# The second graph's gathers wait for TensorE's count of finished blocks

## The reference

```python
# layer 1: neighbours' rows are summed over 200,000 edges
xn = layernorm(x);  x = x + relu(xn @ W + segment_sum((xn @ M)[src], dst))
# layer 2: the gate is a graph attention over 131,072 edges, 16 scores (4 heads x 4 experts)
h     = (xn @ W_gat).reshape(N, 4, 4)
e     = leaky_relu((h * att_src).sum(-1)[src] + (h * att_dst).sum(-1)[dst], 0.2)
alpha = softmax of e over the edges of one destination
agg   = segment_sum(h[src] * alpha, dst)          # then a layernorm, mean over heads
w     = softmax of the two best experts
out   = sum_e w_e * (gelu(xn @ W1[e] + b1[e]) @ W2[e] + b2[e]);  x = x + out
```

## Time and profile before

| | us |
|---|---|
| median of 3 runs | 3728.26 |
| lowest and highest | 3717.64 and 3728.26 |
| profiled execution, its own time | 3704.7 |
| its span, first to last instruction | 3703.5 |
| its mean granted TensorE clock | 0.87 of 2.4 GHz |

### The profile page before, as it was taken

The page is one execution under the profiler, slowest core; times in us unless marked ns, Lnnn a source line. Parts: engine busy times, 40 slices in busy tenths (PEclk is TensorE's granted clock), DMA queues, the critical chain, the costliest instruction groups (busy, mean ns, idle before and its releaser), DMA issues.

```text
span 3703.5 us, 43100 instructions
## 1 busy us (share of the span) xinstructions
PE 2698.6 (73%) x13434; PEld 1984.5 (54%) x13459; DVE 2187.1 (59%) x5820; ACT 900.4 (24%) x1563; POOL 2365.8 (64%) x2799
## 2 busy tenths in 40 slices
PE   2565767778767777677778877777867888788935
PEld 1343545555544545455555555555646766566924
DVE  6677667777765555555455554554123757566957
ACT  3000111111112222211111111111323544344623
POOL 4666666666666666556566666668886678878040
PEclk9767979889888889889899999888978989899968
DMA  9686665666666666566666666665131112122146
GB/s 290 210 259 201 185 203 182 205 205 194 192 190 195 201 199 191 184 186 200 196 206 201 206 204 203 204 203 154 29 100 35 49 38 52 32 51 55 42 142 220
DMA packets 476802, 601.20 MB, mean 162 GB/s; under 512 B 72486, under 2 KB 415390, under 8 KB 474526
## 3 DMA queue, kind: packets, MB, share of 16 engines
q1 hardware_dynamic: 378766, 375.94, 31.3%
q0 software_dynamic: 97216, 219.88, 21.6%
q10 hardware_dynamic: 592, 2.64, 0.2%
HBM read 313.06 MB, written 286.79 MB: 162 GB/s over the span
## 4 chain that ended last, share of the span: by engine, by line
PE 28%; DVE 19%; another core or an unknown queue 14%; issue 10%; DMA 2%; ACT 1%; POOL 1%; SPq 0%; DVEq 0%; ACTq 0%; POOLq 0%
PE wide L1635 11%; PE wide L1524 7%; DVE ring L832 6%; PE wide L1584 4%; PE wide L1574 4%; DVE one_hot L765 3%; DVE picked L890 2%; DMA ring<-xn_d,srci 2%; DVE low_hot L879 1%; PE wide L1543 1%; POOL ring L1727 1%; DVE by_row L992 1%; DVE by_row L985 1%; DVE comb L1167 1%
## 5 line engine op out<-in xcount | busy, mean ns | idle before, releaser
L1727 POOL DMA_INDIRECT ring<-xn_d,srci x1611 | 1559.6, 968 | 907.6 <-issue 405.5
L832 DVE SCALAR_TENSOR_TENSOR ring<-ring,same_v,wide 128x256 f32<-128x256 f32 x1610 | 771.4, 479 | 926.5 <-remote 418.0
L1524 PE MATMUL wide<-ring,one_hot 128*128 128x256 f32 x3222 | 956.3, 434 | 374.0 <-DVE ring L832 217.0
L1524 PEld LDWEIGHTS wide<-ring,one_hot 128*128 128x128 f32 x3222 | 664.5, 216 | 625.0 <-DVE ring L832 209.0
L1635 PE MATMUL wide<-tab_parts,low_hot 128*128 128x208 bf16 x6288 | 729.8, 268 | 163.7 <-issue 149.6
L1635 PEld LDWEIGHTS wide<-tab_parts,low_hot 128*128 128x128 bf16 x6288 | 582.1, 103 | 311.5 <-issue 289.5
L1776 POOL DMA_INDIRECT g<-tab_d,srt x500 | 494.5, 989 | 82.2 <-issue 80.9
L1584 PE MATMUL wide<-w2s,hh 128*128 128x256 f32 x1568 | 417.3, 414 | 64.5 <-DVE yo L806 48.9
L1574 PE MATMUL wide<-xt,w1s 128*128 128x512 f32 (+1 forms) x832 | 407.5, 617 | 18.7 <-ACT hh L1253 15.9
L1584 PEld LDWEIGHTS wide<-w2s,hh 128*128 128x128 f32 x1568 | 325.9, 210 | 138.7 <-DVE yo L806 50.3
L1253 ACT ACTIVATE hh<-wide,b1c 128x512 f32<-128x512 f32 (+1 forms) x208 | 137.6, 662 | 1038.7 <-remote 466.3
(11 more groups left out here) (370 smaller groups left out, 1865.4 us busy)
## 6 DMA issues: line engine op xcount, KB each, us to landing
run_d<-ring SPq DMA_DIRECT2D x201, 1024.0 KB
ring<-xn_d,srci POOLq DMA_INDIRECT x1611
y_d<-yo SPq DMA_DIRECT2D x196, 128.0 KB
comb<-y_d SPq DMA_DIRECT2D x28, 896.0 KB
low_row<-low_d SPq DMA_DIRECT2D x13, 1024.0 KB
sum_d<-g SPq DMA_DIRECT2D x15, 768.0 KB
g<-tab_d,srt POOLq DMA_INDIRECT x500
xn_d<-ring SPq DMA_DIRECT2D x7, 896.0 KB, 7.0
```

Source lines behind the costliest of these rows:

```text
L832: dve_at["run", j] = step(V.scalar_tensor_tensor(out=o, in0=ring[:, (j - 1) // JC % RING, (j - 1) % JC, :], scalar=same_v[:, j:j + 1], in1 ...
L1524: mm = T.matmul(bank[pair_bank[p]][:, j % 2 * D:(j % 2 + 1) * D], one_hot[:, j // 4 % 4, j % 4, :], ring[:, j // JC % RING, j % JC, :], st ...
L1727: G.indirect_dma_start(out=ring[:, s, j % JC, :], out_offset=None, in_=xn_d, in_offset=at_rows(srci[:, j:j + 1])).then_inc(sem(f"gather{s} ...
```

## The change

After it, before the memset of every POOL gather with a number above `left` + 12 = 68, POOL waits until `picked` has reached (number - 68) x 122 // 444 + 1. `sum(pool_cols) - left` is 500 - 56 = 444, so 122 finished blocks are spread over 444 gathers: 3.64 gathers to a block. Gather 69 asks for 1 finished block, gather 100 for 9, gather 160 for 26, gather 256 for 52, and the last, 499, for 119 of the 131. The number and order of all instructions stay as they are.

```diff
 BLOCK_BANK = (4, 6, 0, 2)
 PAUSE = 280
+LOCK_FREE = 12
+LOCK_BLOCKS = 122
...
             for k in range(pool_cols[c]):
                 j = c * FC + k
                 before_it = sum(pool_cols[:c]) + k
+                if before_it > left + LOCK_FREE:
+                    G.wait_ge(sem("picked"), (before_it - left - LOCK_FREE) * LOCK_BLOCKS // (sum(pool_cols) - left) + 1)
                 pause_once()
                 if before_it < left and ahead_of[before_it] > 0:
                     G.wait_ge(sem("y_done"), ahead_of[before_it])
```

## The result

The changed kernel takes 3611.5 us (median of 4 runs, 3607.5 to 3613.7) against 3723.0 us before (4 runs, 3701.9 to 3728.3): a ratio of 0.971, 95% interval 0.967 to 0.975.

What follows compares the result with a forecast made beforehand. PE's blocks, starved while POOL gathers, were taken as the bound; 85 us up to block 22 plus 663 after make 748 against 784, 36 less, so 3728.3 becomes 3692 us; range 3635 to 3755.

Steps and rivals of the forecast that it cites:

- where the wait begins to hold: At 2756 us POOL has issued 101 gathers and PE 10.7 blocks; gather 100 asks for 9, so holding starts there.
- a wait that is met costs nothing: POOL's 431 memsets with one more semaphore: at most 73 us of POOL's time, taken as 0.
- the price of a gather under pacing: PE time per gather above 4.37 us a block: 0.88 us up to block 22, 0.52 after; ends 0.12 and 0.88.
- my 3668: Forecast for the profiled execution: 3704.7 us less 36 us, from 748 us against 784 between 2756 and 3540 us.
- the 0.88: Price in us of each of 41 gathers up to block 22, kept from the 87.67 us stretch; 36.1 us in all.
- my four prices, 0.88 down to 0.52: PE time per gather in four gathering stretches of the kernel before: 0.88, 0.66, 0.59, 0.52 us; 0.63 over all.
- a queue of 64 instructions: TensorE's queue: a pause might store up to 64 of a block's 96 instructions, bringing the sum nearer the first rival.
- The first rival: Short pauses reset PE to 0.12 us a gather; POOL's rate bounds: 652 us, 132 less, 3596; chance 0.14.
- Conservation: Each gather costs PE its mean 0.63 us wherever it stands: 778 against 784 us, 6 less, 3722; chance 0.22.
- the slower rival: Sparse gathers hurt PE like dense ones, 7.5 us a block: 864 us, 80 more, 3808; chance 0.20.
- the 20 I had named: POOL's waits for PE summing to under 20 us would mean the forecast is wrong: conservation or the first rival.
- The pieces of 1 to 4 us: POOL's memset line should wait for PE in many such pieces, instead of 72.4 us for stored sums.

Runs made afterwards that it cites:

- kind C: Chips on which the kernel before takes 3151 and 3154 us; the changed kernel against it there measured 1.0002.
- kind B: The chip on which the kernel before takes 3552 us; the changed kernel against it there measured 1.0022.
- kind A: Chips on which the kernel before takes about 3720 us, that of the first profile included; the changed kernel against it measured 0.971.

## Why the prediction was wrong, point by point

**Right.** What bounds the part (PE, held up while POOL gathers), where the wait begins to hold (near gather 100), no wait of DVE for gathers in the changed trace, the last gather some 50 us ahead of the last block's end, the untouched parts before and behind, and the sign. That PE is short "of instructions" is a reading: shown is that it waits for nothing that the profile has. That a wait that is met costs nothing holds on kind C (0.9991 for 431 of them) and not on kind B (1.0085).

**The step that failed** is the price of a gather under pacing: I took 0.88 us for the 41 gathers up to block 22 and 0.52 us for the 359 after it. The changed trace gives, by the same sum, (94.31 - 73.9) / 61 = 0.33 us for the first and (269 - 195.5) / 174 = 0.42 and (260.61 - 201.8) / 166 = 0.35 us for the rest; over all, (623.92 - 107.8 x 4.37) / 401 = 0.38 instead of 0.56. That is 0.18 x 400 = 70 us, against the 61 us by which the profiled execution, 3607.5, lies under my 3668 for it. The worst miss in relation was the 0.88, which I carried over because DVE does no work on chunks up to block 22. That was not what set it: the gathers of the two stretches take the same 0.95 us each (57.05 / 60 and 58.12 / 61), and what differs is that POOL now stops between some of them.

**Why it failed.** I counted what a stop of POOL gives back at its own length: PE runs free in it, and no more. The changed trace shows that a stop gives back several times its length. This is one of them (timelines of POOL, then of PE):

```profile
3053.73 1.20 POOL L1780 DMA_INDIRECT g<-tab_d,srt  x1 [0.16 <-issue]
3055.38 0.33 POOL L1738 MEMSET pause<- 128x280 f32 x1 [0.45 <-remote]
3055.86 0.95 POOL L1780 DMA_INDIRECT g<-tab_d,srt  x1 [0.15 <-POOL pause L1738]
```

```profile
3054.46 0.52 PE L1637 MATMUL wide<-tab_parts,low_hot 128*128 128x208 bf16 x4 [0.38 <-issue]
3055.22 22.14 PE L1637 MATMUL wide<-tab_parts,low_hot 128*128 128x208 bf16 x244 [0.24 <-issue]
3077.59 0.52 PE L1637 MATMUL wide<-tab_parts,low_hot 128*128 128x208 bf16 x4 [0.23 <-issue]
```

POOL stands for 0.45 us, and PE, which had been starting 4 matmuls at a time with gaps between, runs 244 in a row, for 22 us, while the gathers go on; then it starves again. Each of the 27 short stops of this trace has a run of at least 73 matmuls, 7 us, at or right behind it. In the kernel before, from 2700 us to POOL's first pause at 2843 us, the longest run is of 29; later some ten runs of 73 or more come there without a stop. Another stop, at 2775 us, lies where DVE does no work on chunks yet (windows of the 7 us from 2775.15 on, then those of line 1780):

```profile
2775.15:2782.15 7.00, 7.00 (x77) 6.88 (x78) 6.03 (x8) 5.12 (x8) 6.07 (x10) 1.00 0.11 11
...
2775.15:2782.15 7.00, 4.28 (x5) 1.00 0.11 11
```

That is 77 matmuls in 7 us beside 5 gathers, where the kernel before at its pace of 386 in 87.67 us would do 31. So a stop of 0.73 us gave 46 matmuls, 4 us of TensorE. By that one stop 27 of them would give some 110 us, an estimate to set beside the 106 us measured; the later stretches starved less to begin with, and many runs there are longer, so that the two only agree in size.

Over whole stretches the stops show as a longer beat. On kind A PE does 80 / 61 = 1.3 matmuls per gather at a gather each 1.41 us, and in the kernel before 6.4 at 1.46, 9.3 at 1.50, 10.2 at 1.51 and 11.1 at 1.53; in the changed kernel it is 812 / 61 = 13.3 at 1.55, 12.3 at 1.55 and 13.3 at 1.57; unhindered PE would do 17. On kind B it is 8.5 at 1.48 and the full 17.1 to 17.4 at 1.58. So my four prices, 0.88 down to 0.52, went with the beat as much as with the clock, and I saw only the clock. Between the two stretches whose gathers take 0.95 us in both kernels, 0.09 us more per gather is worth 7 matmuls, 0.6 us of TensorE.

In the later stretches part of this may run the other way. Two neighbouring stretches of ten gathers in the kernel before (windows, then those of line 1776):

```profile
3278.70:3294.60 15.90, 14.63 (x155) 13.62 (x155) 15.50 (x24) 9.23 (x16) 14.26 (x20) 1.00 0.16 38
3294.60:3309.40 14.80, 10.85 (x88) 7.03 (x87) 6.08 (x15) 7.65 (x13) 13.13 (x20) 1.00 0.34 103
...
3278.70:3294.60 15.90, 10.61 (x10) 1.00 0.16 38
3294.60:3309.40 14.80, 9.64 (x10) 1.00 0.34 103
```

Where PE runs nearly free, DVE is busy all the time and a gather takes 1.06 us; where PE starves, DVE is mostly idle and it takes 0.96. There the longer beat can be a result of a fast PE as well as its cause. That a longer beat is a cause is shown where it was set from outside: by the memsets on kind B, and by the stops on kind A.

I had quoted the Trainium skill (TensorE: Matmul & The Clock Gate, the table at its head) on a queue of 64 instructions. 64 instructions are 32 matmuls with their weight loads, an estimate by the page, and the runs behind a stop here are of 73 matmuls and more, up to 265 with gathers going on. What that queue can hold doesn't explain them; the hint pointed the right way and no further.

**The rivals.** The first rival (PE hardly starves, 3596) was nearest with 3611. It named the right event, a short stop that resets PE, but took 0.12 us a gather, where 0.38 was measured, and POOL as the bound; blocks of 5.6 to 6.0 us lie close to the 5.5 us of that bound and above it. My argument against it, that a fast PE outruns the wait and falls back, is seen too: the stretch from 2865 to 3134 us has 6.0 us a block and starved spells in it. But falling back is what makes the wait hold again. Conservation (3722) and the slower rival (3808, from 6.75 us a block) are out by the 5.8 us measured. My sign for them was half right: POOL's waits for PE came to 17.5 us, under the 20 I had named, which pointed to the first rival. The pieces of 1 to 4 us that I had named did not come: only one stop is longer than 1 us.

**What stays open.** That the count of blocks itself, and not any stretching of the beat, is needed on the chips of kind A was not shown: the runs with the met waits, with double memsets and with the longer even beat fell on kinds B and C. Which shared thing the indirect DMAs keep from PE is not known. One candidate can be looked at: the profile has a queue of the kind "instruction", q8, with 108 packets in each kernel of 131 blocks and 111 in each of 138, so it seems to bring PE's instructions. These are its lines for the two starved stretches, 2756.00 to 2843.67 us of the kernel before and 2756.00 to 2841.94 us with PAUSE = 200 (packets, MB, share of 16 engines):

```profile
q8 instruction: 3, 0.05, 0.2%
q8 instruction: 1, 0.02, 0.1%
```

At about 1 us a packet that is 3 us and 1 us of transfer in 86 to 88 us, so the length of these transfers is not what holds PE. What happens before or behind them isn't visible. Why chips differ isn't known either. On kind C the whole program is 570 us faster, most of it in the first part, where POOL gathers too.

## What to carry to other kernels

When an engine shows idle time that waits for nothing visible, look at what another engine does on its own clock beside it, and vary that beat by a few per cent before pricing anything: near an edge, the cost per operation is no constant, and an average over the trace says little about a pacing that the trace doesn't contain. A wait on the slower partner's progress is a cheap governor, since it acts only when that one falls behind, and it cost nothing on kind C, where that never happens. A stop can be worth far more than its own length, so look at what the held engine does after it before pricing it. Once the starvation is gone, ask at once who is next: on kinds B and C it was the gathers, and only shifting columns to TensorE turned a fast TensorE into time.

## What the runs showed that I had not expected

- The same kernel takes 3151, 3552 and 3720 us on three kinds of chip, and a change can be worth 3% on one and nothing on the others (0.971, 1.002, 1.000). An experiment on another chip than the prediction's must bring its own run of the kernel before with a profile.
- Beside indirect DMAs of POOL TensorE took up to 52 us for a block that takes 4.3 alone (kind A, a gather each 1.41 us), and beside memsets that kept POOL busy for 81 of 90 us it took 4.3 (kind B).
- Every stop of POOL of 0.35 to 1.06 us went with about 7 us or more in which TensorE had no gap, beside gathers that went on.
- The memset in front of a gather, which looks like waste, sets the beat: 200 columns instead of 280 cost 5.3% on a chip of kind A.
- A starved TensorE also falls to 1.2 GHz (granted clock 0.50 in the 86 us stretch, 0.75 in the kernel before, 0.97 under the waits; all on kind A). On kind B it stayed at 1.00 in a stretch with 8.3 us a block.
